# The second attention layer's bias step on GpSimd, and its turned-block copies on VectorE

## The reference

```python
q = (x @ Wq + bq).reshape(1, B * N, H, hd)            # 1024 queries, H = 16, hd = 16
q = _fq_sym(q * scale, axis=-1); k = _fq_sym(k, axis=-1); v = _fq_sym(v, axis=2)
attn = jax.nn.softmax(jnp.einsum('bhqd,bhkd->bhqk', q, k), axis=-1)
attn = _fq_unsigned(attn, axis=-1)                    # s = max/255; clip(round(a/s), 0, 255) * s
out = jnp.einsum('bhqk,bhkd->bhqd', attn, v)
```

## Time and profile before

| | before |
|---|---|
| median of three runs | 1067.88 us |
| time of the profiled execution | 1065.92 us |
| span of the profiled execution, first to last instruction | 1064.3 us |
| busy in the whole span: TensorE, VectorE, ScalarE, Pool | 720.2, 544.2, 387.1, 324.3 us |
| first and last exponential of attention 2 | 315.65 and 511.08 us after the start |

### The profile page before, as it was taken

How to read it: one execution, slowest core, us unless ns; L and a number is a source line. 1 busy time by engine, 2 the same in 40 slices (tenths; PEclk the granted TensorE clock), 3 DMA queues, 4 the chain that set the end, 5 groups by cost and what they waited for, 6 DMA issues and landing times.

```text
span 1064.3 us, 14257 instructions
## 1 busy us (share of the span) xinstructions
PE 720.2 (68%) x4990; PEld 484.0 (45%) x4990; DVE 544.2 (51%) x1256; ACT 387.1 (36%) x676; POOL 324.3 (30%) x338
## 2 busy tenths in 40 slices
PE   5964929930558787878776595294866239999980
PEld 3433514420435554555653484153435237677660
DVE  3995323246779988989344153727796200000002
ACT  3001113301269989999420132232653022202200
POOL 4720730058306766667205002400000320100005
PEclk9985969975668888888868697597898569999995
DMA  5060236638109989899502425430012130531503
GB/s 191 1 217 1 103 103 200 194 73 81 16 1 189 192 169 188 170 195 174 105 1 94 158 80 183 130 100 1 1 45 114 45 133 1 182 118 64 182 25 118
DMA packets 152028, 115.43 MB, mean 108 GB/s; under 512 B 108908, under 2 KB 138766, under 8 KB 150944
## 3 DMA queue, kind: packets, MB, share of 16 engines
q1 hardware_dynamic: 143256, 93.91, 34.2%
q0 software_dynamic: 7104, 19.42, 7.6%
q10 hardware_dynamic: 1608, 1.32, 0.4%
HBM read 63.98 MB, written 25.46 MB: 84 GB/s over the span
## 4 chain that ended last, share of the span: by engine, by line
PE 29%; DVE 9%; POOL 4%; issue 4%; DMA 4%; ACT 2%; POOLq 0%; DVEq 0%
PE psum L2030 8%; PE psum L2021 7%; PE psum L1394 3%; PE psum L187 2%; PE psum L1661 2%; POOL grouped_x_dram L1526 1%; POOL moe_x_dram L431 1%; PE psum L1409 1%; DMA both<-grouped_y_dram,idx 1%; PE psum L1251 1%; POOL both L474 1%; DVE both L1916 1%; DVE both L1913 1%; PE psum L527 1%; DVE stats L142 1%
## 5 line engine op out<-in xcount | busy, mean ns | idle before, releaser
L1200 DVE TENSOR_REDUCE both<-psum 128x1 f32<-128x1024 f32 x128 | 155.8, 1217 | 16.0 <-PE psum L1010 15.3
L929 POOL TENSOR_SCALAR both<-both 128x1024 f16<-128x1024 f32 x128 | 133.7, 1044 | 98.3 <-ACT both L1094 90.5
L1094 ACT ACTIVATE both<-psum,both 128x1024 f32<-128x1024 f32 x128 | 154.2, 1217 | 7.1 <-DVE both L1201 4.4
L431 POOL DMA_INDIRECT moe_x_dram<-xn,moe_idx_to x48 | 48.1, 1002 | 218.9 <-DVE moe_idx_from L419 204.9
L1010 PE MATMUL psum<-both 128*128 128x512 bf16 x256 | 92.6, 451 | 24.8 <-ACT both L1094 21.4
L2058 DVE COPY both<-psum 128x256 f32<-128x256 f32 (+1 forms) x24 | 10.1, 422 | 183.8 <-PE psum L2030 183.8
L2030 PE MATMUL psum<-both 128*128 128x256 f32 (+1 forms) x384 | 85.5, 381 | 0.0
L1031 PEld LDWEIGHTS psum<-both 128*128 128x128 f16 x1024 | 64.0, 100 | 46.9 <-ACT both L1101 14.7
L1031 PE MATMUL psum<-both 128*128 128x16 f16 x1024 | 69.8, 173 | 19.4 <-DVE xn L1208 8.1
L474 POOL DMA_INDIRECT both<-moe_y_dram,moe_idx_from x48 | 50.3, 1047 | 90.4 <-DMA moe_y_dram<-both 76.4
L2030 PEld LDWEIGHTS psum<-both 128*128 128x128 f32 (+1 forms) x384 | 65.2, 172 | 19.9 <-issue 4.2
(11 more groups left out here) (325 smaller groups left out, 1422.7 us busy)
## 6 DMA issues: line engine op xcount, KB each, us to landing
both<-in_l_experts SPq DMA_DIRECT2D x50, 384.0 KB, 3.9
both<-in_l_experts SPq DMA_DIRECT2D x8, 2048.0 KB, 8.8
grouped_y_dram<-both SPq DMA_DIRECT2D x31, 128.0 KB
grouped_x_dram<-zeros SPq DMA_DIRECT2D x15, 256.0 KB, 2.5
moe_x_dram<-zeros SPq DMA_DIRECT2D x1, 2560.0 KB, 9.1
both<-kpad_dram SPq DMA_DIRECT2D x1, 2048.0 KB, 8.1
both<-grouped_x_dram SPq DMA_DIRECT2D x1, 2048.0 KB, 13.1
both<-moe_x_dram SPq DMA_DIRECT2D x2, 1024.0 KB, 6.9
```

The costliest lines, as they stand in the source:

```text
L431: nc.gpsimd.indirect_dma_start(out=self.x_dram[:, :], out_offset=bass.IndirectOffsetOnAxis(ap=self.idx_to[:, t, k:k + 1], axis=0), in_=xn[ ...
L929: nc.gpsimd.tensor_scalar(r2[n % RSLOTS2], e2[:, n % ESLOTS2, :], 1.0, HALF_BASE, ALU.mult, ALU.add).then_inc(sem("r2_ready"), 1)
L1094: nc.scalar.activation(e2[:, n % ESLOTS2, :], scores_at(n), ACT.Exp, bias=bias2[:, n:n + 1], scale=s2[:, t * H2 + h:t * H2 + h + 1], accum ...
L1200: seq.step(nc.vector.tensor_reduce(nmax2[:, n:n + 1], scores_at(n), AX.X, ALU.max, negate=True))
```

## The change

Two pieces of work in attention 2 go to another engine. The bias step (128 instructions on a 128 x 1 column) goes from VectorE to Pool. The copy of TensorE's turned blocks (32 instructions on 128 x 1024 fp16 out of PSUM) goes from ScalarE to VectorE. On VectorE the copy of round n-5 stands behind top(n), where on ScalarE that of round n-3 stood behind exp(n). On Pool the bias of round n+1 stands ahead of the round step of n.

```diff
-        LAG2, TURN_LAG2, COPY_LAG2 = 6, 4, 3
+        LAG2, TURN_LAG2, COPY_LAG2 = 6, 4, 5
...
         def l1x_rounds_gpsimd(pool):
-            for n in range(H2 * NT):
+            U = H2 * NT
+
+            def exp_bias(n):
+                h, t = n // NT, n % NT
+                pool.wait_ge(sem("nmax2_ready"), n + 1)
+                nc.gpsimd.tensor_scalar(bias2[:, n:n + 1], nmax2[:, n:n + 1], s2[:, t * H2 + h:t * H2 + h + 1], LN255,
+                                        ALU.mult, ALU.add).then_inc(sem("bias2_ready"), 1)
+
+            exp_bias(0)
+            for n in range(U):
+                if n + 1 < U:
+                    exp_bias(n + 1)
                 pool.wait_ge(sem("e2_ready"), n + 1)
...
-            for n in range(U + COPY_LAG2):
-                if n < U:
-                    exp(n)
-                if n >= COPY_LAG2 and turned_by_tensor(n - COPY_LAG2):
-                    copy_T(n - COPY_LAG2)
+            for n in range(H2 * NT):
+                exp(n)
...
             def top(n):
                 dve.wait_ge(sem("scores2_done"), n + 1)
-                seq.step(nc.vector.tensor_reduce(nmax2[:, n:n + 1], scores_at(n), AX.X, ALU.max, negate=True))
-                nc.vector.tensor_scalar(bias2[:, n:n + 1], nmax2[:, n:n + 1], s2[:, t * H2 + h:t * H2 + h + 1], LN255,
-                                        ALU.mult, ALU.add).then_inc(sem("bias2_ready"), 1)
+                nc.vector.tensor_reduce(nmax2[:, n:n + 1], scores_at(n), AX.X, ALU.max, negate=True).then_inc(sem("nmax2_ready"), 1)
...
+            def copy_T(n):
+                dve.wait_ge(sem("rT2_blocks"), tensor_turns(n + 1))
+                if n >= RSLOTS2:
+                    dve.wait_ge(sem("values2_done"), n - RSLOTS2 + 1)
+                nc.vector.tensor_copy(rT2[n % RSLOTS2], bank[7].bitcast(F16)).then_inc(sem("rT2_by_vector"), 1)
...
                 top(n)
+                if n >= COPY_LAG2 and turned_by_tensor(n - COPY_LAG2):
+                    copy_T(n - COPY_LAG2)
```

More of the change, by code:

```diff
@@ L933, in turned2 @@
             if turned_by_tensor(n):
-                eng.wait_ge(sem("rT2_by_scalar"), tensor_turns(n + 1))
+                eng.wait_ge(sem("rT2_by_vector"), tensor_turns(n + 1))
             else:
@@ L1016, in turn @@
                 if tensor_turns(n):
-                    pe.wait_ge(sem("rT2_by_scalar"), tensor_turns(n))
+                    pe.wait_ge(sem("rT2_by_vector"), tensor_turns(n))
                 for j in range(NT):
@@ L1197, in top @@
             def top(n):
-                h, t = n // NT, n % NT
                 dve.wait_ge(sem("scores2_done"), n + 1)
-                seq.step(nc.vector.tensor_reduce(nmax2[:, n:n + 1], scores_at(n), AX.X, ALU.max, negate=True))
-                nc.vector.tensor_scalar(bias2[:, n:n + 1], nmax2[:, n:n + 1], s2[:, t * H2 + h:t * H2 + h + 1], LN255,
-                                        ALU.mult, ALU.add).then_inc(sem("bias2_ready"), 1)
+                nc.vector.tensor_reduce(nmax2[:, n:n + 1], scores_at(n), AX.X, ALU.max, negate=True).then_inc(sem("nmax2_ready"), 1)
             def scale_out(g):
@@ L1220, in l1x_vector @@
                 top(n)
+                if n >= COPY_LAG2 and turned_by_tensor(n - COPY_LAG2):
+                    copy_T(n - COPY_LAG2)
+            for n in range(U - COPY_LAG2, U):
+                if turned_by_tensor(n):
+                    copy_T(n)
             scale_out(H2 // GH2 - 1)
```

## The result

The changed kernel takes 1073.62 us (median of 10 runs, 1071.83 to 1078.13), the kernel before 1070.56 us in the runs taken beside it. The ratio is 1.0041, with a 95% interval from 1.0025 to 1.0057. The forecast was 1058.5 us and a range of 1051 to 1068. The profiled execution took 1078.13 us with a span of 1076.4 us. The difference between the two profiles is therefore larger than the change's effect; they are read here for what happens inside attention 2.

A forecast was written before the change was run, and what follows sets the result against it. ScalarE with its copies (1.41 us a round) was taken as the bound, VectorE (1.38) close. After the change, 1.34 plus 0.05 lost makes 1.39 for 1.462: 8.7 us gained over 121 steps, net 7.8; forecast 1058.5 us, range 1051 to 1068.

The forecast's parts named there:

- Pool's own work: Pool in attention 2: round step 1.04 plus bias step 0.20, 1.24 us a round, below the 1.34 us bound.
- the ring: Exponential, Pool's round step, Pool's bias step, exponential two rounds on: 1.34 us a round, the largest bound after the change.
- the loss of 0.05: Time lost between engines in each round of attention 2, 0.05 us, taken to stay as before the change.
- the stalls: Three scale_out stalls between exponentials, 18.5 us for six steps, to stay and grow by 0.4 us each.
- the copy's cover: Slack for the copy between VectorE's reductions: 0.05 to 0.15 us, gone whenever TensorE is slow.
- VectorE's terms: VectorE after the change: 1.14 us a reduction, copy 693 ns (0.61 beside neighbours), 5.17 us for four rounds.
- ScalarE's terms: ScalarE without its 32 copies needs 1.19 us a round for exponentials and is no bound.
- B: Rival, chance 0.13: bias step on Pool costs twice VectorE's, 0.43 us; no gain in the steps, 1067 us.
- D: Rival, chance 0.12: slower, if Pool's bias step and two hops exceed 0.50 us together; at 0.70 us, 1079.
- C: Rival, chance 0.12: DMA transposes already full at a share of 0.96, half of 7.8 us left, 1062 to 1066.
- E: Rival, chance 0.05: no loss between the engines, 1.31 us a round, 18 us gained, 1049 us.
- The signs: Expected in the trace: exponentials 1.39 us apart, waiting for Pool's bias; Pool over 90% busy; last exponential near 503 us.

The follow-up runs named there:

- the half-step run: Changed kernel with Pool's round step doing only half the columns from round 5 on, so not a complete version; 1066.31 us, ratio 0.9978.

## Why the prediction was wrong, by its own steps

**The step that failed is the sentence "Pool's own work, 1.04 + 0.20, is 1.24 us and lies below that".** It is 1.04 + 0.09 + 0.26 + 0.09 = 1.48 us, more than any other bound. The kind of sum was right, an engine's whole stream in a round; its size was not. Two terms in it are off. The bias step takes 0.264 us, inside my bounds of 0.10 and 0.29 but not my 0.20. And I added no gaps around Pool's instructions, only 0.02 us in the ring. The earlier trace rows could have warned me: Pool sits idle 0.24 us there between its own L240 and L242. Put into the forecast's own sum, a bound of 1.484 with the loss of 0.05 makes a round 1.534 in place of 1.39, so 121 x (1.462 - 1.534) = -8.7 us in place of 8.7 gained. The direction followed from the size: before's steps already averaged 1.462. With the stalls as measured, 2.4 us shorter, the stage gets 6.3 us longer, and in the two profiles it got 6.3 us longer. Between the medians it is 3.1 us, 10.9 from the 7.8 us that were forecast as gained. The rest of the 15.1 us between 1058.5 and 1073.62 is none of the change's: before's median rose by 2.7 us with more runs, and 1058.5 lay 1.6 us under what the sum gives against the median.

**Pool's ring** was costed at 1.34 us a round and is 1.41. Its 1.38, 1.04 and 0.04 were right; the bias step and the gap weren't. It doesn't bind in the full change, where the stream is longer, but it does when fewer bias steps are on Pool.

**The loss of 0.05 us** between the engines held nearly to the digit: 1.537 - 1.484 = 0.053 us, 6 us in the stage. That is luck, for its cause is largely new. I had written that the copy's cover was 0.05 to 0.15 us and that TensorE's values would wait for it; then I priced that at nothing. Moving the copy ahead of the reduction takes the loss to 0.022. Beside it, on a pace of 1.48, a lost step is never made up.

**VectorE's terms** were right: 0.68 for 0.69 us for the copy, and 1.13 for 1.14 us from one reduction to the next, so the overlap of 0.08 us that I took over from the copies holds for reductions too. The bound is 5.12 us in four rounds for 5.17. I first read 1.20 off the half-step run, where the reductions also wait for scores, and so the sums for VectorE in the later expectations are too high by 0.07 us for each reduction that has no bias step behind it.

**ScalarE's terms** were right: exponentials at 1.19 where nothing holds them.

**The stalls.** I expected 0.4 us more at each; the six steps took 15.7 us after 18.1, 2.4 us less in all. The copy's leaving ScalarE isn't the reason: with the copies moved and the bias steps left the six steps take 18.6 us, with the bias steps moved and the copies left 15.2. They are short where all bias steps are Pool's; why isn't shown.

**The rivals.** B had the right engine and a price of 0.43 us for the bias step, giving 1067. The rule of the Trainium skill behind it (GPSIMD Engine Reference, § 4.1 Engine selection), which keeps elementwise work on VectorE, pointed the right way. Its factor of about two is for two-input steps, and one-input steps it calls roughly line-rate; by the trace this step is 0.264 us on Pool and 0.21 on VectorE, a quarter more. D wanted more than 0.50 us from step and hops together and priced the ring; they are 0.09 + 0.26 + 0.04 = 0.39. (Its "in place of 0.24" should read 0.26, by the ring's own terms.) What decided was neither, but Pool's stream. C is not borne out as a bound of the changed kernel: its DMA share over the stage fell from 0.96 to 0.90, and with half round steps on Pool the same transposes ran in less time, at a share of 0.98, and 1.01 with the copy ahead; with 112 transposes it is 1.06. So 0.96 isn't full. As a bound at a faster pace it stays possible: at the mean step of 1.401 TensorE's waits for transposes are 42.7 us, twice before's 21.2. E's faster pace never came.

**The signs** named ahead: the exponentials do wait for Pool's bias (39.1 us). Pool's busy share came to 150.6 of 184 us, 82%, not over 90%. The gaps don't count as busy: even at its full pace Pool shows 1.31 of 1.484 us, 88%. The last exponential starts at 521.5 us, not 503.

What stays open: what the 0.09 us ahead of each Pool instruction are, and what the remaining losses are made of. TensorE's lower clock (a mean of 0.85 over the stage) and its waits for transposes may be in them; no run tells the two apart.

## What to carry to other kernels

Before work is moved to an engine that looks two thirds busy, add up that engine's whole stream for one round, gaps included, and compare it with the pace, not with its idle share: here Pool had 1.466 - 1.04 = 0.42 us a round beside its round step, and a bias step of 0.26 us with two gaps of 0.09 asks for 0.44, before any gain in pace is counted. A tiny instruction in an in-order queue costs what it waits for and what stands behind it: one round further ahead on Pool the same bias step cost 18 us more, and ahead of the exponential on ScalarE nearly 50 more. And put work for a third engine (here the copy that TensorE waits for) ahead of the long instruction in the queue, if its input is ready.

## What the runs showed of the hardware

- In these rounds a Pool instruction starts 0.09 us after the recorded end of the one before it, where both carry waits, even fulfilled ones (397.91 + 0.26 to 398.26); the pair of steps takes 1.484 us.
- On VectorE a reduction of 128 x 1024 fp32 from PSUM takes 1.22 us, and one that nothing holds starts 1.13 us behind the one before it, 0.08 us before that ends (332.45, two in 2.34 us).
- A step on a 128 x 1 column with a column as scalar operand takes 0.264 us on Pool, 0.21 us on VectorE, and 0.29 us on ScalarE, where the exponential behind it is moved by 0.20 us only.
- VectorE copies a 128 x 1024 fp16 block out of PSUM in 0.68 us, ScalarE in 1.01 us.
